# A gated delta rule layer: raw keys with one factor per token, and level sums taken out of products with a standing identity by ScalarE

## The reference, cut to what matters

```python
mixed = silu(causal_conv1d(hidden_states @ w_qkv, conv_w))   # four taps
q, k, v = split(mixed)
q = l2norm(q); k = l2norm(k)          # x * rsqrt(sum(x*x) + eps), per token and head
def step(St, inp):                    # a scan over the 512 tokens
    q_t, k_t, v_t, g_t, b_t = inp
    St = St * exp(g_t)
    v_old = k_t . St
    delta = (v_t - v_old) * b_t
    St = St + outer(k_t, delta)
    return St, q_t . St
core = core * rsqrt(mean(core*core) + eps) * norm_weight * silu(z)
out = core @ w_out
```

## Time and profile before

| what | value |
|---|---|
| median of 3 runs | 3311.82 us (3311.48 to 3314.59) |
| the profiled execution: span from first to last instruction | 3310.8 us |
| busy share of the span: PE, PEld, DVE, ACT, POOL | 97%, 64%, 74%, 47%, 56% |
| mean granted clock of TensorE (share of full speed) | 0.992 |
| the delta rule's slots, in the span | about 70 to 2470 us |

### The profile page before, as it was taken

How to read it: one execution, slowest core, us unless ns; L and a number is a source line. 1 busy time by engine, 2 the same in 40 slices (tenths; PEclk the granted TensorE clock), 3 DMA queues, 4 the chain that set the end, 5 groups by cost and what they waited for, 6 DMA issues and landing times. The chain is left out here.

```text
span 3310.8 us, 60236 instructions
## 1 busy us (share of the span) xinstructions
PE 3215.4 (97%) x20576; PEld 2131.6 (64%) x20576; DVE 2448.0 (74%) x3686; ACT 1550.6 (47%) x4983; POOL 1859.5 (56%) x1824
## 2 busy tenths in 40 slices
PE   5899999999999999999999999999979999999999
PEld 2577777777777777777777777777754444454444
DVE  6899999999999999999999999999940011034453
ACT  2465656565656565556555655565531000022232
POOL 2677777777777777777777777777730000011132
PEclk8999999999999999999999999999999999999999
DMA  2133333323333233323333332333325222211001
GB/s 94 48 77 84 77 72 74 85 70 74 80 84 75 69 80 76 77 70 83 80 75 73 80 81 70 77 79 81 81 62 207 76 102 102 76 39 64 0 13 39
DMA packets 423119, 248.75 MB, mean 75 GB/s; under 512 B 306688, under 2 KB 372352, under 8 KB 417280
## 3 DMA queue, kind: packets, MB, share of 16 engines
q1 hardware_dynamic: 421520, 237.81, 27.5%
q10 hardware_dynamic: 1296, 7.08, 0.5%
HBM read 156.39 MB, written 71.57 MB: 69 GB/s over the span
## 5 line engine op out<-in xcount | busy, mean ns | idle before, releaser
L736 PE MATMUL acc<-xT,wc 128*128 128x512 f32 x2048 | 934.8, 599 | 2.7 <-PEq L112 2.0
L736 PEld LDWEIGHTS acc<-xT,wc 128*128 128x128 f32 x2048 | 369.7, 190 | 372.6 <-issue 372.0
L1015 DVE SCALAR_TENSOR_TENSOR d_conv<-acc,wc,d_conv 128x511 f32<-128x511 f32 (+2 forms) x768 | 566.8, 738 | 41.8 <-ACT d_conv L1190 32.6
L749 PE MATMUL acc<-wc,xT 128*128 128x256 f32 x2048 | 473.4, 384 | 0.0
L749 PEld LDWEIGHTS acc<-wc,xT 128*128 128x128 f32 x2048 | 379.1, 190 | 46.2
L1541 PE MATMUL acc<-t_area 128*128 128x512 f32 x768 | 332.5, 592 | 1.6 <-ACT t_area L1990 1.6
L634 POOL TENSOR_TENSOR d_bf<-d_kks,d_gam 128x512 f32<-128x512 f32 x128 | 160.6, 1277 | 294.9 <-ACT d_kks L1234 294.9
L2047 POOL TENSOR_SCALAR t_veps<-t_mv 128x1 f32<-128x1 f32 x32 | 9.7, 303 | 547.0 <-DVE t_mv L1786 547.0
L1048 DVE STREAM_TRANSPOSE d_em<-d_dm 128x1024 f16<-128x1024 f16 x256 | 314.5, 1228 | 2.2
L1776 DVE TENSOR_TENSOR t_x<-acc,t_x 128x512 f32<-128x512 f32 x16 | 11.1, 691 | 392.3 <-PE acc L1541 392.3
L1055 DVE TENSOR_TENSOR d_zm<-d_tz,cons 128x512 f16<-128x512 f32 x384 | 259.0, 674 | 52.0 <-PE d_tz L799 47.0
(11 more groups left out here) (228 smaller groups left out, 7002.3 us busy)
## 6 DMA issues: line engine op xcount, KB each, us to landing
d_decay<-decay_rows SPq DMA_DIRECT2D x64, 512.0 KB, 5.2
v_rows<-d_vb SPq DMA_DIRECT2D x256, 128.0 KB, 2.3
d_vn<-v_rows SPq DMA_DIRECT2D x64, 512.0 KB, 3.7
core_rows<-d_ob SPq DMA_DIRECT2D x1024, 32.0 KB, 1.7
t_area<-core_rows SPq DMA_DIRECT2D x30, 1024.0 KB, 4.8
wc<-in_w SPq DMA_DIRECT2D x96, 256.0 KB, 3.2
d_qn<-d_qf SPq DMA_DIRECT2D x1024, 16.0 KB, 1.8
t_x<-in_x SPq DMA_DIRECT2D x4, 1024.0 KB, 9.2
```

The costliest lines, as they stand in the source:

```text
L736: last = nc.tensor.matmul(bank(TILE[j])[:, :], wtile(j, k), xT[:, k, r % B * S:(r % B + 1) * S], start=k == 0, stop=k == KT - 1)
L749: last = nc.tensor.matmul(bank(f"z{j}")[:, i * GV * P:(i + 1) * GV * P].rearrange("p (h n) -> p h n", h=GV), xT[:, k, r % B * S + (2 * j + ...
L1015: nc.vector.scalar_tensor_tensor(c[:, d:S], bank(TILE[j])[:, 0:S - d], tap(j, KS - 1 - d), c[:, d:S], ALU.mult, ALU.add).then_inc(taps, 1)
```

## The change

1. **Raw keys.** `silu` writes the keys straight into `kT`, and `k_turn`, `kk` and `kq` use them unnormalised; `khat_turn`, `copy_kT` and `kraw` go. POOL `k_norm` makes two powers of the sum of squares per token, -1 and +0.5 (8 elements in place of 4). The copies that follow carry the factor: `normal_k`, `copy_kk` and `copy_kq` scale by the power -1 and so go in four pieces, one per chunk; a new ACT step `scale_v` multiplies the values of a chunk by the power +0.5 (four pieces of 128 x 256, in place). PE `solve(s, 0)` waits for `scale_v` where it waited for the load of the values.
2. **Standing identity.** `zm` is filled with the identity once. DVE `level_z` writes only where the mask holds (`copy_predicated`, its mask read as integers), so the identity stays, and the product of `em` and `zm` is already the level's sum. The six DVE additions of an item (`level_d` for levels 0 to 3, `level_e` for 4 and 5) go; ACT copies the sums out of PSUM: `copy_d` for all six levels, in one full-size instruction each, and `copy_e` for levels 4 and 5. The sign of B moves into the constants.
3. **Order.** The new ACT steps stand in ACT's hand-written order at places of their own; PE's order only loses `khat_turn`, DVE's only the additions.

The diff, without constants, declarations and renamed semaphores:

```diff
 # POOL
-                wait(pool, khat_ready, at(back(n, 1), NC, NC))
-                nc.gpsimd.tensor_tensor(rk[:, :], rkt[:, :], cons[:, C_POW:C_POW + NC], ALU.pow).then_inc(rk_ready, 1)
+                wait(pool, kqs_ready, at(back(n, 2), NC, NC))
+                wait(pool, v_scaled, at(back(n, 2), NC, NC))
+                nc.gpsimd.tensor_tensor(rk[n[1] % 2][:, :, :], bc(rkt[:, :], 2), cons[:, C_KPOW:C_KPOW + 2 * NC].rearrange("p (e c) -> p e c", e=2),
+                                        ALU.pow).then_inc(rk_ready, 1)
 # PE
-                turn(bank("k_turn"), kraw, k_turned)
-            def khat_turn(n):
-                pe.wait_ge(khat_ready, at(n, NC, NC))
-                ring_free(n, "khat_turn")
-                turn(bank("khat_turn"), khat[n[1] % 2], khat_turned)
+                turn(bank("k_turn"), kT[third(n)], k_turned)
             def kk(n):
-                pe.wait_ge(kT_ready, count(n))
+                pe.wait_ge(silued, nth(n, "silued", 0))
             def level_z(m, l):
...
-                elif l < 5:
-                    pe.wait_ge(d_added, at(m, 4, l))
                 else:
-                    pe.wait_ge(d_copied, at(m, 3, 2))
+                    pe.wait_ge(d_copied, at(m, LEVELS, l))
             def solve(s, c):
-                    pe.wait_ge(v_moved, at(s, 80, 80))
+                    pe.wait_ge(v_scaled, at(s, NC, NC))
 # DVE
-                nc.vector.memset(zm[l][:, :], 0.0).then_inc(zeros_set, 1)
+                nc.vector.tensor_copy(zm[l][:, :].rearrange("p (a n) -> p a n", n=P), bc(cons[:, C_ID:C_ID + P], GV * NC)).then_inc(zm_set, 1)
             def level_z(m, l):
-                nc.vector.tensor_tensor(even(zm[l], l), packed(tz, l), bc(mask, GV * NC), ALU.mult).then_inc(z_ready, 1)
-            def level_d(m, l):
-                nc.vector.tensor_tensor(even(dm, l), packed(td, l), even(dm, l), ALU.add).then_inc(d_added, 1)
-            def level_e(m, l):
-                nc.vector.tensor_tensor(odd(e, l), packed(te, l), odd(e, l), ALU.add).then_inc(e_added, 1)
+                nc.vector.copy_predicated(even(zm[l], l), bc(mask, GV * NC), packed(tz, l)).then_inc(z_ready, 1)
 # ACT
+            def scale_v(s):
+                act.wait_ge(v_moved, at(s, 80, 80))
+                for c in range(NC):
+                    v = vn[s[1] % 2][:, :, :, :].rearrange("p a (h c) j -> p (a h) c j", c=NC)[:, :, c, :]
+                    nc.scalar.activation(v, v, ACT.Copy, scale=rk[s[1] % 2][:, 1, c:c + 1]).then_inc(v_scaled, 1)
             def copy_kk(n):
-                nc.scalar.activation(kks[:, :], bank("kk")[:, :], ACT.Copy).then_inc(kk_copied, 1)
+                for c in range(NC):
+                    nc.scalar.activation(chunk(kks, c), chunk(bank("kk"), c), ACT.Copy, scale=rk[n[1] % 2][:, 0, c:c + 1]).then_inc(kk_copied, 1)
-            def copy_d(m, l, n):
+            def copy_d(m, l):
                 act.wait_ge(d_done, at(m, LEVELS, l + 1))
-                rows = slice((n * 2 + 1) * (2 << l), (n * 2 + 2) * (2 << l))
-                nc.scalar.activation(even(dm, l)[rows, :, n, :], packed(td, l)[rows, :, n, :], ACT.Copy).then_inc(d_copied, 1)
+                nc.scalar.activation(even(dm, l), packed(td, l), ACT.Copy).then_inc(d_copied, 1)
+            def copy_e(m, l):
+                act.wait_ge(e_done, at(m, 2, l - 3))
+                act.wait_ge(d_done, at(m, LEVELS, l + 1))
+                nc.scalar.activation(odd(em[m[1] % 2], l), packed(te, l), ACT.Copy).then_inc(e_copied, 1)
 # ACT's order in a slot
                     read_q(f, 2, 0)
-                    copy_d(s, 5, 0)
+                    scale_v(s); copy_d(s, 5); copy_e(s, 5)
                     silu(n, 0)
...
                     k_square(n)
+                    copy_d(m, 0)
                     solved(s, 0)
...
                     first_state(s)
+                    copy_d(m, 1)
                     o_scale(f, 0)
                     o_scale(f, 1)
                     copy_kq(m)
                     first_output(s)
-                    copy_kT(n)
+                    copy_d(m, 2)
                     solved(s, 1)
                     read_q(s, 1, 1)
                     read_q(s, 1, 0)
                     copy_kk(n)
+                    copy_d(m, 3)
                     first_tap(n, 2)
...
                     silu(n, 2)
-                    copy_d(m, 4, 1)
-                    copy_d(m, 4, 0)
+                    copy_d(m, 4); copy_e(m, 4)
```

More of the change, by code:

```diff
@@ L45 @@
 C_RMS = C_L2 + NC
-C_END = C_RMS + NC
+C_KPOW = C_RMS + NC
+C_END = C_KPOW + 2 * NC
 DECW = S
@@ L981, in slot @@
                     level_d(m, 2)
-                if project:
-                    khat_turn(n)
                 if recur:
@@ L1112, in slot @@
                     decays(n, 0)
-                if recur:
-                    level_e(s, 5)
                 if finish:
@@ L1137, in slot @@
                 if invert:
-                    level_d(m, 0)
                     flip_v(m)
@@ L1143, in slot @@
                     convolve(n, 3, 2)
-                if invert:
-                    level_d(m, 1)
                 if project:
@@ L1156, in slot @@
                 if invert:
-                    level_d(m, 2)
                     flip_d(m, 2)
@@ L1162, in slot @@
                     next_state(s, 1, 1)
-                if invert:
-                    level_d(m, 3)
                 if recur:
@@ L1177, in slot @@
                     flip_q(m)
-                    level_e(m, 4)
             long_slots(dve, slot)
@@ L1194, in silu @@
                 if j == 0:
-                    wait(act, k_turned, count(n, 1))
+                    wait(act, ks_s, at(back(n, 3), 3, 3))
                 if j >= 2:
@@ L1198, in silu @@
                 v = vraw
-                out = (kraw[:, :], qT[third(n)][:, :], v[:, 0, :], v[:, 1, :])[j]
+                out = (kT[third(n)][:, :], qT[third(n)][:, :], v[:, 0, :], v[:, 1, :])[j]
                 nc.scalar.activation(out, conv_of(TILE[j])[:, :], ACT.Silu).then_inc(silued, 1)
@@ L1220, in q_square @@
                 squares(lambda c: qn[:, :, c, :], lambda c: qn[:, :, c, :], qss, q_squares, scale=(RMS_EPS * HD) ** 0.5)
-            def copy_kT(n):
-                act.wait_ge(khat_turned, count(n))
-                nc.scalar.activation(kT[third(n)][:, :], bank("khat_turn")[:, :], ACT.Copy).then_inc(kT_ready, 1)
+            def scale_v(s):
[3 more added lines that the diff above has]
+                    nc.scalar.activation(v, v, ACT.Copy, scale=rk[s[1] % 2][:, 1, c:c + 1]).then_inc(v_scaled, 1)
             def b_high(n, h):
@@ L1251, in copy_kq @@
                 wait(act, p_ready, at(back(m, 1), GV, GV))
-                nc.scalar.activation(kqs[:, :], bank("kq")[:, :], ACT.Copy).then_inc(kqs_ready, 1)
-            def copy_d(m, l, n):
+                for c in range(NC):
+                    nc.scalar.activation(chunk(kqs, c), chunk(bank("kq"), c), ACT.Copy, scale=rk[m[1] % 2][:, 0, c:c + 1]).then_inc(kqs_ready, 1)
+            def copy_d(m, l):
                 act.wait_ge(d_done, at(m, LEVELS, l + 1))
-                rows = slice((n * 2 + 1) * (2 << l), (n * 2 + 2) * (2 << l))
-                nc.scalar.activation(even(dm, l)[rows, :, n, :], packed(td, l)[rows, :, n, :], ACT.Copy).then_inc(d_copied, 1)
+                nc.scalar.activation(even(dm, l), packed(td, l), ACT.Copy).then_inc(d_copied, 1)
[3 more added lines that the diff above has]
+                nc.scalar.activation(odd(em[m[1] % 2], l), packed(te, l), ACT.Copy).then_inc(e_copied, 1)
             def read_q(s, c, h):
@@ L1299, in slot @@
                 if recur:
-                    copy_d(s, 5, 0)
+                    scale_v(s)
+                    copy_d(s, 5)
+                    copy_e(s, 5)
                 if project:
@@ L1355, in slot @@
                 if invert:
-                    copy_d(m, 4, 1)
-                    copy_d(m, 4, 0)
+                    copy_d(m, 4)
+                    copy_e(m, 4)
             long_slots(act, slot)
```

64 lines of the change are left out of this document (33 added, 31 removed).

## The result

| | median, us | runs | ratio to before (95%) |
|---|---|---|---|
| before, same chip | 3312.21 | 3311.48 to 3314.59 | |
| after | 3380.85 | 3380.38 to 3381.61 | 1.0204 (1.0190 to 1.0219) |

The changed kernel is 2.0% slower, 5 us under the forecast. Its profiled span is 3379.4 us, 68.6 more than before, at the same mean clock of 0.992. From the first to the last `k_turn` on PE the 63 slots take 2358.7 us (79.84 to 2438.56) where they took 2291.8 (80.16 to 2371.91): 67.0 of the 68.6 lie there.

What follows compares the result with a forecast made beforehand. PE's instruction stream was taken as the bound. Waits of +0.51 and +0.61 us in 62 slots (69.4), with 6, 1 and -2, made 74.4 us more: 3386 us, +2.2%; own range 3362 to 3408, 8 in 10 for 3345 to 3430.

Steps and rivals of the forecast that it cites:

- The gate wait: PE before solve(s, 1): copy_d(m, 1) ahead of o_scale makes PE stand 0.98 us a slot, solve 0.51 late beside before.
- six steps of the chain: From PE level_d(m, 1) through ScalarE's copy, o_scale, o_gate, flip_o and residuals to solve(s, 1): 6.60 us against PE's 5.62.
- The level wait: PE before level_z of level 4: copy_d(m, 3), queued behind the four copy_kk pieces, comes 0.61 us late each slot.
- The slot: A slot without a weight load, 36.52 us before, grows by 1.12 to about 37.6.
- The slots with a weight load: In 15 slots scale_v delays refine by 1.0 us, taken as 0.4 each: 6 us in all, bounds 0 and 16.
- The head: Filling zm with the identity instead of zeros, by six copies of 1024 elements: 0 to 3.4 us, taken as 1.
- the first three slots: The first slots, where PE waits for the chain of keys anyway, lose khat_turn: -2 us.
- the rival of two passes: VectorE's predicated copy in level_z takes 1.23 us in place of 0.65: 68 us more, 3454; chance 0.10.
- The signs I had named: Profile after: PE idle near 100 us, about 60 before solve, 38 before level_z; VectorE busy time down some 220.
- The faster rival: PE's shorter stream wins: if neither copy came late, 30 us of transposes fall off, 3282 us; chance 0.08.
- the hand-off to `read_k`: VectorE's flip_d, level_z(m, 3), next_state end at about 1580.6, where PE reaches read_k at 1580.63: no wait.
- each 0.1 us off the chain is 6 us: Shortening the 6.60 us path from level_d(m, 1) to solve(s, 1); below 6.1 a gain if level 4 doesn't wait either.

Runs made afterwards that it cites:

- sum1_on_vector: Changed kernel with the level 1 sum copied by VectorE, where its addition had stood, instead of ScalarE: 3325.3 us.
- raw_keys_alone: Kernel before with only the raw keys part (factors in the copies, scale_v, no second transposes), VectorE keeping its additions: 3332.5 us.
- sums13_on_vector: Changed kernel with the sums of levels 1 and 3 copied by VectorE, ScalarE keeping the other four levels: 3308.5 us.
- dead_transposes: Changed kernel with the four transposes of khat put back at their old place on PE, into a bank nobody reads: 3382.5 us.
- raw_keys_late_v: Kernel before with only the raw keys part, and scale_v moved behind the level 5 copy on ScalarE: 3316.2 us.

## Why the prediction was right, and where its terms were off

**The gate wait.** Predicted 0.98 us, measured 0.98. All six steps of the chain came within 0.03 us of their values, and `o_scale` came 0.91 later against `level_d` than before. sum1_on_vector, which takes only that copy out, gives 0.92 a slot back. The mechanism is shown.

**The level wait.** Predicted 0.61, measured 0.68 to 0.69: `kk` starts 1.74 after `solve` instead of 1.68, mostly because a `solve` that has stood still lets the next instruction go after 0.55, not 0.45. The four pieces held ScalarE 1.02 us (1585.13 to 1586.15), as the row of before said. The estimate of 1.17 from the figures of the Trainium skill (ScalarE: Activation LUTs, What ACT_TABLE_LOAD costs) was too much here; the measurement decides.

**The slot.** Predicted 36.52 + 1.12, "about 37.6"; measured 37.76, +1.24. Over 45 slots the 0.12 makes 5.4 us too little.

**The slots with a weight load** are the term that was mis-sized. Predicted +1.12 + 0.4 us each, measured +0.80 (12.0 us over 15): about 11 us too much. `refine` goes there by the later of two paths. One is PE's own order with its waits: without a weight load `refine` comes 30.52 us after `k_turn` before the change and 31.75 after it. The other is the loaded taps: in the changed kernel the tap that waits for them comes 28.00 us after `k_turn` (28.13 before), `scale_v` and the copy follow, and `refine` comes at 31.91, 3.91 after the tap. So what `scale_v` costs in these slots is the 0.16 by which the second path is the later one. In raw_keys_alone, where PE is not late, the same path costs the full difference, 32.44 against 31.01, or 1.4 where I had put 1.0 us before VectorE's earlier request. I had added the wait at `refine` to the two others as if PE came there at its old pace.

**The rest.** The head came 0.3 us earlier where I had +1, and the first three slots together 0.7 shorter where I had 2. Of the 62 slots that I counted 60 lie before the last `k_turn`; the part behind it is 1.9 longer, where the other two were to give 2.2. With the 5.4 that the slots without weights gave more and the 11 that those with weights gave less, this makes the 5.8 us between the forecast of 74.4 and the measured 68.6. The forecast is as near as that in part by luck, since the two largest errors have opposite signs.

**copy_predicated** takes what the multiplication took, so the rival of two passes fell. The rows by line, after, over the whole span:

```profile
L1051 DVE CAST_PREDICATED d_zm<-cons,d_tz 128x512 f16<-128x512 int32 x384 | 265.4, 691 | 161.6 <-PE d_tz L797 155.0
```

**The signs I had named** came true: PE's idle time 84 us (near 100), 48.7 before `solve` and 33.2 before `level_z` with the named releasers (60 and 38), `o_scale` 0.49 after its copy (0.5), VectorE down by 257 us over the span (220), and idle 1.7 us ahead of each `flip_o` (2).

**A sentence that was wrong.** The faster rival, 3282, let 30 us of transposes fall off as soon as neither copy came late. sums13_on_vector is that kernel, and it took 3308.5. I had seen the hand-off to `read_k`, "in time, with nothing to spare", and did not carry it into that price: a chain with nothing to spare becomes the bound as soon as PE's work beside it is cut. The rule that "each 0.1 us off the chain is 6 us" ends there too. That the slot of the changed kernel came out near all the same is because its wait for the residual is longer than the transposes; dead_transposes shows that they then count for nothing either way.

What stays open: why the loaded taps come 1.36 us sooner after `k_turn` when the quarter tile is moved, and with it why PE's wait before `attend` in the slots with weights (9.3 us in raw_keys_late_v) goes. ScalarE's copy for `attend` stands behind that tap, but no run took it apart.

## What to carry to other kernels

An engine that is busy 99% of a stretch is not by that the bound of each part of it: work taken from it gives nothing where another engine's chain beside it is as long, and the gain comes only when other work of the engine is put in its place. Before moving a step to an idler engine, look at what is queued behind its new place: a copy of 0.6 us ahead of `o_scale` cost 0.98 us a slot through four engines, on an engine that was 59% busy. Waits in one slot need not add up: where two paths lead to an instruction only the later one counts, so price each wait against the pace that the others leave, and after taking one away look at which path comes last.

## What the runs showed of the hardware that had not been expected

- `solve(s, 1)`, four single-precision matmuls, costs more than its wait when its operand comes late: it lets its successor start after 0.55 us in the changed kernel, 0.45 before, and its record is 0.71 instead of 0.61. It is the same 0.55 in sums13_on_vector, where it comes only 0.06 late. `level_z` in half precision, 0.69 late in the changed kernel, shows no such difference (0.24 to the next start).
- Four transposes of 128 x 128 in single precision hold PE for 0.47 us beside other work, and for nothing inside a wait (3380.9 without, 3382.5 with).
- A masked copy on VectorE out of PSUM, 128 x 512 with the mask in integers, takes 691 ns; the multiplication of the same operands took 674 in the kernel before (257.6 us in 382, from 110 to 2430 us).
